# A router one slot later: moving the weight squares, the key projection's copy and the row turning in a hand-scheduled attention and expert kernel

## The reference

```python
kv  = ctx @ W_k.T + b_k                      # 512 x 128 a batch
out = layernorm(x) @ kv                      # einsum bij,bjd->bid
sim = (out @ kv.T) * 512 ** -0.5
sim = (sim - mean) * rsqrt(var + 1e-6) * gamma + beta
x   = x + softmax(sim)
n   = layernorm(x)
top2 scores of n @ Wg.T, softmax over the two -> weights w
y   = sum over e of w_e * (silu(n @ W1[e].T) * (n @ W2[e].T)) @ W3[e].T
return x + y
```

## Time and profile before

| | |
|---|---|
| median of 3 runs | 422.46 us (419.2 to 424.24) |
| the profiled execution's own time | 422.72 us |
| its span, first to last instruction | 420.7 us |
| TensorE busy over the span | 357.0 us (85%) |
| VectorE, ScalarE, GpSimd busy | 269.0, 266.5, 164.9 us |
| mean granted TensorE clock | 0.895 of full |

### The profile page before, as it was taken

The page is one execution under the profiler, slowest core; times in us unless marked ns, Lnnn a source line. Parts: engine busy times, 40 slices in busy tenths (PEclk is TensorE's granted clock), DMA queues, the critical chain, the costliest instruction groups (busy, mean ns, idle before and its releaser), DMA issues.

```text
span 420.7 us, 7558 instructions
## 1 busy us (share of the span) xinstructions
PE 357.0 (85%) x2009; PEld 229.8 (55%) x2009; DVE 269.0 (64%) x658; ACT 266.5 (63%) x457; POOL 164.9 (39%) x185
## 2 busy tenths in 40 slices
PE   2868699696965277899999999999999999999982
PEld 0433465564664155455566666666666666666650
DVE  0163655647657947999876676676676676676670
ACT  2177665667665927889766666666666666666660
POOL 1115353553750440455434334334434434434322
PEclk9998859679555569899999999999999999999998
DMA  7955979874998020234454354354454354354333
GB/s 231 404 233 192 321 246 277 286 233 156 287 286 333 1 77 25 37 66 66 87 102 73 81 100 76 79 100 73 81 101 78 76 101 80 75 99 80 78 47 50
DMA packets 21831, 57.57 MB, mean 137 GB/s; under 512 B 4832, under 2 KB 4960, under 8 KB 20256
## 3 DMA queue, kind: packets, MB, share of 16 engines
q0 software_dynamic: 8736, 20.53, 27.3%
q1 hardware_dynamic: 13056, 36.56, 25.4%
HBM read 38.17 MB, written 18.91 MB: 136 GB/s over the span
## 4 chain that ended last, share of the span: by engine, by line
PE 54%; DVE 7%; issue 3%; ACT 2%; DMA 1%; POOLq 0%; POOL 0%; ACTq 0%; DVEq 0%
PE bank L1031 30%; PE bank L1063 15%; PE bank L1022 4%; PE bank L1049 3%; DVE stage L804 2%; DVE Wp L684 2%; PE bank L888 1%; ACT stage L568 1%; DMA out<-kvj_s,sidx 1%; DVE stage L835 1%; DVE kvg_s L841 1%; DVE x_s L865 1%; POOLq L65 0%; POOL w3rs L439 0%; PE bank L1002 0%
## 5 line engine op out<-in xcount | busy, mean ns | idle before, releaser
L835 DVE SCALAR_TENSOR_TENSOR stage<-W,w3sc,stage 128x512 f16<-128x512 f16 x117 | 84.1, 747 | 8.7 <-ACT stage L568 8.5
L1063 PE MATMUL bank<-stage,n_s 128*128 128x512 f16 (+1 forms) x351 | 83.2, 382 | 3.7 <-DVE n_s L859 2.2
L1031 PE MATMUL bank<-Wp,kvg_s 128*128 x480 | 79.4, 316 | 2.2 <-DVE kvg_s L841 2.2
L568 ACT ACTIVATE stage<-W,w3sc 128x512 f16 x117 | 80.3, 718 | 0.0
L1031 PE MATMUL bank<-Wp,kv_s 128*128 x456 | 74.3, 312 | 2.0 <-DVE kv_s L841 2.0
L446 POOL DMA_INDIRECT out<-oT_s,sidx x20 | 35.7, 1785 | 78.0 <-ACT oT_s L593 70.5
L1031 PEld LDWEIGHTS bank<-Wp,kvg_s 128*128 128x128 f16 x480 | 47.3, 99 | 29.9 <-issue 4.5
L1031 PEld LDWEIGHTS bank<-Wp,kv_s 128*128 128x128 f16 x456 | 44.4, 98 | 26.7 <-issue 3.0
L446 POOL DMA_INDIRECT out<-kvj_s,sidx x19 | 32.5, 1711 | 64.4 <-ACT kvj_s L593 61.7
L859 DVE TENSOR_TENSOR n_s<-bank,n_s 128x384 f16<-128x384 f32 x39 | 21.7, 557 | 55.4 <-ACT n_s L581 55.4
L1063 PEld LDWEIGHTS bank<-stage,n_s 128*128 128x128 f16 (+1 forms) x351 | 34.3, 98 | 37.4 <-issue 4.9
(11 more groups left out here) (155 smaller groups left out, 512.3 us busy)
## 6 DMA issues: line engine op xcount, KB each, us to landing
Wp<-in_w SPq DMA_DIRECT2D x8, 1408.0 KB, 7.1
W<-in_w SPq DMA_DIRECT2D x8, 768.0 KB, 7.0
stage<-in_xT SPq DMA_DIRECT2D x4, 1024.0 KB, 7.2
x_s<-in_x SPq DMA_DIRECT2D x16, 256.0 KB, 6.1
out<-x_s SPq DMA_DIRECT2D x16, 256.0 KB, 5.8
n_table<-n_s SPq DMA_DIRECT2D x16, 256.0 KB, 3.4
stage<-in_ctxT SPq DMA_DIRECT2D x1, 768.0 KB, 8.2
x_s<-n_table,gidx POOLq DMA_INDIRECT x39, 4.3
```

Source lines behind the costliest of these rows:

```text
L568: eng.activation(w3p[t % 2][:, c * D:(c + 1) * D], W3[:, bass.ds(e * W3N + c * D, D)], ACT.Copy, scale=w3sc[:, bass.ds(e, 1)]).then_inc(s_ ...
L835: eng.scalar_tensor_tensor(w3p[r][:, W3N + c * D:W3N + (c + 1) * D], W3[:, bass.ds(e * W3N + c * D, D)], w3sc[:, bass.ds(e, 1)], w3p[r][:, ...
L1031: mm = eng.matmul(bank[2 * which + r][:, 0:H], n_, w_, start=(c == 0 and k == 0), stop=(c == DC - 1 and k == 2))
L1063: mm = eng.matmul(ybank(t - 1)[:, :], h_, w_, start=(c == 0 and k == 0), stop=(c == HC - 1 and k == 2))
```

## The change

Five things are moved; nothing is computed otherwise.

- The router comes one slot later: scores on TensorE and their reading on VectorE have lag 4 in place of 3. Router weights, edl and the router store follow in slots 0 and 1 of the next batch. One slot, (4,3), is added at the end.
- On ScalarE the weight squares (and the copies w12_high of slots 17 and 18) stand at the front of a slot, behind the copy of the turned rows.
- On ScalarE oT's copy stands at the front of slot 2, ahead of the weight squares and the exponential.
- On TensorE turn_n is the last thing in a slot, behind outs, gram_outs, keys and turn_keys; in the draining slots it stays first.
- SyncE's router store leaves the end of a batch and stands at the front of slot 1.

```diff
-        def batches(slot, after=None, weights=None):
-            for b in range(B + 1):
-                for q, (b_, i) in enumerate(body_slots(b)):
+        def batches(slot, weights=None):
+            for b in range(B + 2):
+                for q, (b_, i) in enumerate(body_slots(b)[:1 if b > B else TPB]):
                     slot(b_, i)
                     if weights:
                         weights(TPB * b + q)
-                if after:
-                    after(b)
...
 SyncE
             def slot(b, i):
+                if i == 1 and real(b - 2):
+                    router_store(b - 2)
...
-            batches(slot, router_store, weights)
+            batches(slot, weights)
+            router_store(B - 1)
...
 ScalarE, slot(b, i), behind the copy to nT_s
+                if i == 0 and real(b - 2):
+                    router_exp(b - 2)
+                if i == 2 and real(b + 1):
+                    o_evac(b + 1)
+                weights(TPB * (b + 1) + i - (TPB - 1))
                 if real(b):
...
-                if i == 2 and real(b + 1):
-                    o_evac(b + 1)
...
-                if real(b3) and i3 == 3:
-                    eng.wait_ge(s_dl, b3 + 1)
...
-            batches(slot, None, weights)
+            batches(slot)
+            router_exp(B - 1)
...
 VectorE, slot(b, i)
+                if i == 0 and real(b - 2):
+                    router_weights(b - 2)
...
-                b3, i3 = lag(b, i, 3)
+                b3, i3 = lag(b, i, 4)
...
                     if i3 == 3:
                         router(b3)
-                        if b < B:
-                            router_weights(b3)
...
 TensorE, slot(b, i)
-                wait(eng, s_sc, n - 3)
+                wait(eng, s_sc, n - 4)
...
-                b3, i3 = lag(b, i, 3)
+                b3, i3 = lag(b, i, 4)
...
-                if not draining:
-                    turn_n(*lag(b, i, 2))
                 if i == 1 and real(b + 1):
                     outs(b + 1)
...
                 if i == 0 and real(b + 1):
                     turn_keys(b + 1)
+                if not draining:
+                    turn_n(*lag(b, i, 2))
```

More of the change, by code:

```diff
@@ L311, in weights @@
                     load_w12(2 + n // 2)
-                if n > 2 * E - 5:
+                if 2 * E - 5 < n < 2 * E + 4:
                     load_w3(n - 2 * E + 4)
@@ L333, in router_store @@
             def router_store(b):
[L335 to L340, removed]
-            batches(slot, router_store, weights)
+                eng.wait_ge(s_w2, b + 1)
+                eng.wait_ge(s_wi, b + 1)
+                eng.dma_start(nrows[bass.ds(b * TPB, TPB), :, D:ROW].rearrange("g p k -> p g k"),
+                              wrow[:, bass.ds(b * TPB, TPB), :]).then_inc(s_wst, 16)
+            batches(slot, weights)
+            router_store(B - 1)
             eng.wait_ge(s_zr, 1)
@@ L513, in slot, with router_exp @@
                     kvj_evac(b + 1)
-                if real(b3) and i3 == 3:
-                    eng.wait_ge(s_dl, b3 + 1)
-                    cols = bass.ds(b3 * TPB, TPB)
-                    eng.activation(edl[:, cols], dlt[:, cols], ACT.Exp).then_inc(s_ed, 1)
+            def router_exp(b):
+                eng.wait_ge(s_dl, b + 1)
+                cols = bass.ds(b * TPB, TPB)
+                eng.activation(edl[:, cols], dlt[:, cols], ACT.Exp).then_inc(s_ed, 1)
             def squares(k, h):
```

## The result

| | before | after |
|---|---|---|
| median of 20 runs each, same chip | 422.89 us | 424.56 us |
| ratio, 95% interval | | 1.005 (1.0026 to 1.0074) |
| profiled execution | 422.72 us | 426.14 us |
| two batches (row squares of slot (0,3) to (2,3)) | 54.40 us | 56.06 us |
| from there to the last row squares | 21.37 us | 20.58 us |

The change makes the kernel slower, by 0.5%, where 0.3% faster was forecast. The time lies in the range of the forecast, but the direction is the other one. Of the 3.4 us between the two profiled executions 2.7 are there at the one-hot; the unchanged code behind it took 290.1 us before and 290.7 after (the span, 420.7 and 424.1 us, less the one-hot). So the first 158 us hold the answer, as said.

The account below looks back on a forecast made before the run. The prediction took weight-load waits to bind the batches at 26.0 us. Last row squares at 118.6 plus drain 10.7 put the one-hot at 129.3 against 130.64, 1.3 us gained: 421.1 us, range 416 to 426.

Parts of the forecast that it names:

- The bound and where the gain is decided: Only the first 158 us can move; each microsecond the one-hot at 130.64 moves is one in the time.
- The 23.9 us left by TensorE's wait: Batches: without TensorE's 3.3 us wait for turned rows, the 27.2 us cycle could take 23.9 at least.
- The weight squares at the front: ScalarE's squares wait for loads, forming a loop of 13.0 us per two slots; batch 26.0 us, down from 27.2.
- landing 7.0: Load loop term: each weight load lands 7.0 us after issue, within the 13.0 us turn.
- The forecast's own sign of being wrong: Listed signs against it: no ScalarE idle before weight squares, a batch under 25 or over 27 us, among others.
- The rival of the late loads: Weight loads 3 to 7 land later; at 8.4 us, 7.0 us more, 428.4 us in all; chance 0.11.
- Each microsecond of landing is paid five times: Squares of loads 3 to 7 wait in turn, so each microsecond of landing counts five times, before never.
- oT ahead of the exponential, cost 0: ScalarE stands still until outs is done, but load waits cover it; 0 taken, up to 2.1 us a batch uncovered.
- Turning last: the 3.3 us: Turning last and scores one slot later remove TensorE's 3.3 us wait; some returns at VectorE's score copy.
- The last batch: From row squares at 98.3, the last x1 waits for the output store; last row squares at 118.6, 3.2 us earlier.
- The drain, 10.7 us: Last row squares to one-hot takes 10.7 us instead of 8.80, 1.9 more for the added slot.
- The tail at full clock (0.20): Rival: TensorE keeps full clock in the drain, 2.2 us less, 1.5 more if the store lands early, 417.7; chance 0.20.

Follow-up runs that it names:

- e1: The changed kernel with ScalarE's weight squares put back at the end of its slot; 416.72 us, 0.9841 of the kernel before.
- e3: The changed kernel, squares still in front, with SyncE issuing weight loads at the front of its slot, ahead of the n_s store; 418.88 us, 0.9885 of the kernel before.
- e11: e6 with SyncE also issuing the weight loads at the front of its slots; 414.63 us, 0.9803 of the kernel before.
- e7: The changed kernel with squares at slot's end, oT's copy behind the row squares, turning ahead of outs; router lag kept; 420.02 us, 0.9948 of before.
- e8: The changed kernel with weight squares at the slot's end and turning ahead of outs, oT's copy in front; 415.62 us, 0.9853 of before.
- e9: The changed kernel with weight squares at the slot's end and oT's copy behind the row squares, turning last; 425.27 us, 1.0067 of before.
- e4: The changed kernel with the turning last on TensorE in the draining slots too; 423.13 us, 0.9999 of the kernel before.
- e2: The kernel before with only the weight squares (and slots 17 and 18's scaled copies) moved to the front; 422.53 us, 1.0039 of before.
- e6: e1 with turning last in the draining slots and expert 0's low weights ahead of the reading in the added slot; 415.44 us, 0.9828 of before.
- e10: e8 with turnings behind scores in the draining slots and expert 0's low weights ahead of the reading; 416.97 us, 0.9863 of before.
- e5: The changed kernel with SyncE issuing the xT load behind the weight load instead of one slot ahead; 423.89 us, 1.0042 of before.

## Why the prediction went wrong, step by step

**The bound and where the gain is decided: right.** The part behind the one-hot differs by 0.7 us. The matmuls' wait for nT is gone and one for the score copy (4.7 us) has come; the squares start on the landing of loads 3 to 7.

**The 23.9 us left by TensorE's wait: right.** e1 has 24.4 us a batch, e3 24.6, e11 24.4.

**The weight squares at the front: the step that failed, in its term "landing 7.0".** The form of the loop was right and so were its other terms: 2.65 us to the row squares (forecast 2.6) and 3.47 to 3.63 to the issue (3.4). The landings of loads 4 to 7 were 8.6, 6.7, 8.8 and 7.0 where 7.0 was taken for each. Summed over four turns the landings are 3.1 us more than forecast, the issues 0.6, the rest 0.4: 56.1 us for 52.0. The first squares were 0.6 us early (43.09 for 43.7), so the row squares of (2,3) came at 101.80 in place of 98.3. That is 3.5 of the 4.1 us between the forecast one-hot and the real one, and it turns a gain of 1.3 into a loss. The forecast's own sign of being wrong, a batch over 27 us, came: 28.03. The load of 7.1 us was load 4 of the old order, where the xT load had been issued 7.7 us ahead of it; the new order brought the two to 5.3 us (and 6.1 for load 6), and the old landing was carried over. The rival of the late loads had named the very two, behind xT; it was priced as if all five were late at 8.4 us, and so given 0.11. Two of five late at 8.7 was the case between, and it was not worked out: 421.4 + 2 x 1.7 = 424.8 us, slower (the profiled execution took 426.14). The forecast also took some 2 us and 436 GB/s from the Trainium skill (DMA: Bandwidth & Descriptors, Anatomy of one DMA), 5.3 us for this load. That section gives them for DMAs issued by GpSimd, and this load is issued by SyncE. The measured 6.7 to 8.8 us of the changed kernel decide, and none of loads 4 to 7 in any run landed in less than 6.3.

**"Each microsecond of landing is paid five times": right in kind.** e1 shows the other side: a landing of 9.2 us cost 1.2 there.

**oT ahead of the exponential, cost 0: the cost was right, the worth was missed.** The forecast asked only what it delays, not what it releases. It is worth 1.0% (e7 to e8) to 2.2% (e9 to e1), hidden in the change by the loads. Without the squares in front the change is 1.6% faster than the kernel before (e1), which the prediction's 23.9 us did imply: two batches at 24.4 against 27.2 is 5.7 us.

**Turning last: the 3.3 us.** What took the 3.3 us away is that the scores no longer use a copy of their own slot; the place of the turning gives nothing that can be told with oT in front (e8 beside e1).

**The last batch: right.** Row squares of (2,3) to the last ones took 20.58 us (forecast 20.3), and the last x1 began 0.05 us behind the landing of the output store, as forecast. A part of the fit is luck: the store was issued 4.29 us behind the row squares of slot (3,1) (110.66 to 114.95), where 3.8 was forecast, and took 6.4 us for 6.8.

**The drain, 10.7 us: right.** 10.99 measured, 1.72 to 1.85 us for each group of scores. e4 shows that it was avoidable: with the turning last there too, the drain is 8.78.

**The tail at full clock (0.20): did not come.** TensorE's granted clock from 100 to 131 us was 0.61, against 0.56 before, and 0.50 in e1 and e11, which are 1.6 and 2.0% faster than the kernel before all the same.

## What to carry to other kernels

Before moving the reader of a load forward in an in-order queue, ask what in that queue leads to the next load's issue: if the reader stands ahead of it, issue, landing and reader form a loop whose length is mostly latency outside the reader's own engine (here 10 to 12 of the 13 to 15 us of a turn). Write that sum with the landing of each load as its neighbours will make it, not with one landing from the old trace, and cut the loop where it is cheapest, here by leaving the reader behind the work that others wait for, or by issuing the loads ahead of the store. Test a change of several moves as a square of its parts: here one move hid the worth of the others, and another, the turning last, was harmless only beside a third, oT in front.

## What the runs showed of the hardware that was not expected

How long a 1.4 MB load takes went with what was issued ahead of it. Loads 4 to 7 of the kernel before, the change and all eleven experiments:

| what was issued near it | loads | landing |
|---|---|---|
| xT load 7.4 to 8.4 us ahead (loads 4 and 6; before, e2, e7, e9) | 8 | 6.8 to 7.4 us |
| xT load 5.3 to 6.1 us ahead (loads 4 and 6; the change, e1, e4, e6, e8, e10) | 12 | 8.2 to 9.7 us |
| xT load 0.5 us behind (loads 4 and 6; e3, e5, e11) | 6 | 6.3 to 7.0 us |
| no xT load within 8 us ahead (loads 5 and 7; before, the change, e2, e4, e5, e7, e9) | 14 | 6.7 to 7.2 us |
| the same (loads 5 and 7; e1, e3, e6, e8, e10, e11) | 12 | 7.2 to 8.8 us |

In the change the xT loads took 6.0 and 8.0 us themselves, so they were in flight for 0.7 and 1.9 us more when the weight load was issued. That short overlap goes with 1.5 to 2 us on the load behind, while a load right behind it costs the weight load nothing. The last row shows that xT is not the only thing that can make a load late: in these kernels the weight load before stood 9.4 to 11.7 us ahead, and 15 us ahead in the change, but in e9 and e7 loads that stood 9.6 and 10.6 us behind the one before landed after 7.2 and 6.7 us. What makes the difference was not tried.

The granted clock of TensorE from 46 to 100 us was 0.84 in e1 and e11, and 0.74 and 0.77 in the change and e3. TensorE was busy for 40.39 us with 178 matmuls there in e1, for 41.65 us with 160 in the change. But e6, with the same code there as e1, had 0.74, and e8 and e10, with the same code as each other, had 0.76 and 0.84. So the clock differs between executions of the same code, and that it rises when the waits are removed is not shown. In both pairs the execution with the higher clock has the shorter two batches, by 1.7 and 2.6 us. How much of that the clock makes, no run separates.
